# Two-stream attention block: the query features move to the other stream's fourth PSUM bank, and ScalarE's order of two activations is swapped

## What is computed

```
q, k, v = out@Wq+bq, out@Wk+bk, out@Wv+bv            # split into 16 heads of 8
favor(x) = [exp(u - h), exp(-u - h)] / sqrt(8)        # u = xs@omega, h = 0.5*sum(xs*xs), xs = x * 8**-0.25
Qf, Kf = favor(q), favor(k)
S_t = S_{t-1} + Kf_t v_t^T;  z_t = z_{t-1} + Kf_t     # causal, over the 1024 tokens
a_t = (Qf_t S_t) / (Qf_t z_t + 1e-6)
h = LN(out + a@Wo + bo);  out = LN(h + relu(h@W1+bf1)@W2 + bf2)
```

## Time and profile before

| | |
|---|---|
| median of 3 runs | 2047.53 us (2046.19 to 2049.01) |
| profiled execution, its own time | 2053.53 us |
| its span, first to last instruction | 2051.6 us |
| busy, share of the span | PE 82%, DVE 76%, POOL 48%, ACT 43%, PEld 61% |
| mean granted TensorE clock | 0.903 of full speed |
| attention slots | about 641 to 1880 us of the span |

### The profile page before, as it was taken

How to read it: one execution, slowest core, us unless ns; L and a number is a source line. 1 busy time by engine, 2 the same in 40 slices (tenths; PEclk the granted TensorE clock), 3 DMA queues, 4 the chain that set the end, 5 groups by cost and what they waited for, 6 DMA issues and landing times. The chain is left out here.

```text
span 2051.6 us, 69397 instructions
## 1 busy us (share of the span) xinstructions
PE 1680.2 (82%) x28443; PEld 1259.8 (61%) x28445; DVE 1554.3 (76%) x3835; ACT 883.3 (43%) x1642; POOL 983.6 (48%) x1045
## 2 busy tenths in 40 slices
PE   5655555469937999999999989999989999995798
PEld 4332334359935666766666766666766666663798
DVE  2899965359976878878888878888868878885675
ACT  2555555446623444444444434444434444442321
POOL 0677747769953224234234224224224224223797
PEclk7877765579977999999999999999999999997899
DMA  7400011122230000000000000000000000000001
GB/s 202 86 0 0 0 24 34 34 63 63 64 111 2 3 3 3 3 3 3 3 3 3 3 4 3 3 3 3 3 4 3 3 3 3 3 3 1 16 31 37
DMA packets 60732, 42.92 MB, mean 21 GB/s; under 512 B 19720, under 2 KB 54800, under 8 KB 59952
## 3 DMA queue, kind: packets, MB, share of 16 engines
q1 hardware_dynamic: 47504, 25.35, 4.7%
q0 software_dynamic: 4352, 8.99, 1.3%
q10 hardware_dynamic: 8608, 4.67, 0.9%
HBM read 24.22 MB, written 14.77 MB: 19 GB/s over the span
## 5 line engine op out<-in xcount | busy, mean ns | idle before, releaser
L368 POOL TENSOR_TENSOR at_rstd<-at_mv,const 128x4 f32<-128x4 f32 x96 | 19.5, 203 | 570.0 <-DVE at_mv L362 569.9
L1622 PE MATMUL psum<-attn_w,at_qa 128*128 128x128 f32 x1536 | 184.1, 278 | 0.0
L1614 PE MATMUL psum<-at_vT,attn_w 128*128 128x512 f32 x384 | 180.5, 613 | 1.4 <-ACT at_vT L1427 0.9
L1622 PEld LDWEIGHTS psum<-attn_w,at_qa 128*128 128x128 f32 x1536 | 175.2, 192 | 2.7 <-issue 0.6
L1431 ACT ACTIVATE at_qa<-psum,attn_bf 128x512 f32<-128x512 f32 x192 | 132.0, 687 | 90.2 <-PE psum L1614 90.2
L1326 DVE TENSOR_SCALAR at_kb<-at_kf,const 128x512 f32<-128x512 f32 x192 | 157.9, 882 | 0.0
L1332 DVE STREAM_TRANSPOSE at_vb<-at_vT 32x512 uint32<-32x512 uint32 x192 | 134.7, 702 | 1.9
L1848 PE MATMUL psum<-tilesT,ti_masked 128*128 128x128 f32 x1024 | 119.9, 279 | 12.9 <-POOL ti_masked L1810 12.9
L1848 PEld LDWEIGHTS psum<-tilesT,ti_masked 128*128 128x128 f32 x1024 | 117.8, 195 | 14.6 <-issue 14.6
L1556 PE MATMUL psum<-at_state,at_qa 64*64 64x36 f32 x3072 | 116.8, 242 | 9.6 <-issue 9.2
L1435 ACT ACTIVATE at_qa<-at_qf,const 128x512 f32<-128x512 f32 x192 | 122.3, 710 | 0.0
(11 more groups left out here) (303 smaller groups left out, 4315.2 us busy)
## 6 DMA issues: line engine op xcount, KB each, us to landing
ex_xs<-sorted_x SPq DMA_DIRECT2D x80, 65.0 KB
x<-in_L_attn_x ACTq DMA_DIRECT2D x8, 512.0 KB, 8.5
ex_feats<-token_y SPq DMA_DIRECT2D x4, 1024.0 KB, 8.1
out<-x SPq DMA_DIRECT2D x16, 256.0 KB, 2.3
expert_w<-in_L_ffn_w SPq DMA_DIRECT2D x1, 2048.0 KB, 9.5
attn_w<-in_L_attn_W SPq DMA_DIRECT2D x2, 768.0 KB
token_y<-ex_y,ex_place POOLq DMA_INDIRECT x72
sorted_x<-ex_spare SPq DMA_DIRECT2D x1, 1040.0 KB, 8.3
```

Source lines behind the costliest of these rows:

```text
L1614: mm(bank(f.s, c), k.w1[:, f.l, c * P:(c + 1) * P], hT[f.s][:], start=True, stop=True).then_inc(hid_ready, 1)
L1622: last = mm(bank(f.s, 1)[:, c * D:(c + 1) * D], hidden[f.s][:, t, c * P:(c + 1) * P], k.w2[:, f.l, t, :], start=(t == 0 and c == 0), stop= ...
```

## The change

Two things are changed in `attention`. The query features are accumulated in `bank(1 - s, 3)`, the fourth bank of the other stream, in place of `bank(s, 3)`. With that, `sums` no longer writes to the bank that the exponential reads, and PE's wait for `qf_ready` moves from before the first sums to before the fourth hidden product, the next write to that bank. On ACT the copy of the transposed rows (`hT`) comes ahead of the query exponential. No arithmetic is added or removed.

```diff
@@ ScalarE @@
                         act.wait_ge(kt_ready, n + 1)
                         nc.scalar.activation(flat(kt[s][:]), bank(s, 2), ACT.Copy).then_inc(vk_taken, 1)
+                    if f:
+                        act.wait_ge(hT_ready, f.count + 1)
+                        nc.scalar.activation(hT[f.s][:], bank(f.s, 2), ACT.Identity, bias=col(B1, f.l), scale=col(G1, f.l)).then_inc(hT_taken, 1)
+                    if a:
                         act.wait_ge(feat_ready, n * 2 + 2)
                         if l == 0 and a.before:
                             act.wait_ge(outcome_free, a.turn - 1)
-                        nc.scalar.activation(qf[s][:], bank(s, 3), ACT.Exp, bias=feature_bias[:, 0, l:l + 1]).then_inc(qf_ready, 1)
-                    if f:
-                        act.wait_ge(hT_ready, f.count + 1)
-                        nc.scalar.activation(hT[f.s][:], bank(f.s, 2), ACT.Identity, bias=col(B1, f.l), scale=col(G1, f.l)).then_inc(hT_taken, 1)
+                        nc.scalar.activation(qf[s][:], bank(1 - s, 3), ACT.Exp, bias=feature_bias[:, 0, l:l + 1]).then_inc(qf_ready, 1)
@@ TensorE @@
-                        mm(bank(s, 3), wu[0][:, l, :], xT[s][:], start=True, stop=False)
+                        mm(bank(1 - s, 3), wu[0][:, l, :], xT[s][:], start=True, stop=False)
...
                         pe.wait_ge(kq_taken, n * 2 + 2)
-                        mm(bank(s, 3), cst(k, "half"), sqq[s][:], start=False, stop=True).then_inc(feat_ready, 1)
+                        mm(bank(1 - s, 3), cst(k, "half"), sqq[s][:], start=False, stop=True).then_inc(feat_ready, 1)
...
                         pe.wait_ge(vk_taken, n * 2 + 2)
-                        pe.wait_ge(qf_ready, n + 1)
                         sums(s, 0)
                         sums(s, 1)
                     if f:
                         pe.wait_ge(hT_taken, f.count + 1)
                         for c in range(GC):
+                            if a and c == 3:
+                                pe.wait_ge(qf_ready, n + 1)
                             mm(bank(f.s, c), k.w1[:, f.l, c * P:(c + 1) * P], hT[f.s][:], start=True, stop=True).then_inc(hid_ready, 1)
```

## The result

| | before | changed |
|---|---|---|
| median of 6 runs each, same chip | 2048.27 us (2045.37 to 2053.09) | 2038.34 us (2031.34 to 2040.28) |
| profiled execution, its span, mean clock | 2053.53, 2051.6, 0.903 | 2037.89, 2036.0, 0.908 |

The ratio is 0.9943, with the 95% interval from 0.9923 to 0.9962: faster, by 9.9 us of medians. The forecast was 2041.3 us in a range of 2036.0 to 2047.0, for a gain of 6.2. That is a ratio of 0.9970, which lies just outside the interval: the gain was larger than forecast, and not by noise alone. Two later comparisons gave the changed kernel 0.9931 and 0.995 of the kernel before, and one of the kernel before against itself gave 1.0003.

What follows compares the result with a forecast made beforehand. PE was taken to bound attention (1111.82 of 1187.00 us busy). 26 ordinary slots x 0.24 us = 6.2 us, set against the median before of 2047.53 us, gave 2041.3 us, range 2036.0 to 2047.0.

Steps and rivals of the forecast that it cites:

- An ordinary slot: Attention slot outside the groups bound by POOL and DVE: hidden product starts 0.24 us earlier, in 26 of 47 slots.
- The exponential and the new wait: On ACT and PE: later exponential still precedes the ReLUs, and the wait before the fourth hidden product is met; cost nothing.
- The groups of three: Seven groups, 21 attention slots, held by DVE and POOL at 52.24 us from first to third normalisation: no gain.
- holes for issue: PE's idle stretches in dense runs of small passes, 0.8 us on average; may open or close, counted as nothing.
- All slots gaining: Rival: groups of three not bound, all 47 slots give 0.24 us, 11.3 us in all, 2036.2 us; chance 0.09.
- Swallowed: Rival: copy starts no earlier or holes take the gain back; 2.6 us down to nothing, 2044.9 to 2047.5; chance 0.26.
- slower: Rival: shifted instruction stream opens new 0.8 us holes in ordinary slots, 10.4 us against 6.2, 2051.7 us; chance 0.08.
- (1): PE in attention: the first sums no longer wait for ACT and start right behind the transposes.
- (2): ACT in attention: the copy of the rows starts 0.05 us behind the transposes, ahead of the exponential.
- (5): Ordinary slots 0.24 us shorter; groups of three still 52.2 us from first to third normalisation, PE waiting longer for rows there.
- (3): Hidden product 0.05 us behind the copy, with new PE waits for the copy of about 0.1 us per ordinary slot.
- (6): PE's holes for issue keep the same total; the prediction is wrong if this fails by more than some us.

Runs made afterwards that it cites:

- number 2: Changed kernel with ACT's old order (exponential first, then the copy), bank and PE wait as changed: 2037.44 us, ratio 0.9982.
- number 1: Kernel before with ACT's order alone swapped (copy, then exponential), bank and PE wait as before: 2127.7 us, ratio 1.0422.
- number 8: Changed kernel with PE's wait for the query exponential before the first hidden product in place of the fourth: 2065.7 us, ratio 1.007.
- number 9: Changed kernel with POOL's two residual passes moved behind the feed-forward input's passes and held until DVE's masked copies are made: 2025.77 us, ratio 0.9905.
- number 3: Changed kernel with one more, long-met wait on PE before the first sums in each slot: 2036.41 us, ratio 0.9972.
- number 4: Kernel before without PE's wait for the copy of the transposed keys ahead of the sums: 2043.14 us, ratio 1.0006.
- number 6: Changed kernel with POOL's two residual passes moved behind the first reciprocal deviation and the two passes after it, without a hold: 2098.73 us, ratio 1.023.
- number 10: Changed kernel with POOL's residual passes moved later, these and the feed-forward input's passes held until DVE's masked copies are made: 2027.39 us, ratio 0.992.

## Why the prediction was right, and what it missed

**An ordinary slot: right.** Predicted 0.24 us, with the copy 0.05 behind the transposes and the hidden product 0.05 behind the copy; measured 0.24, with 0.04 and 0.05. The two halves are shown apart by the floor: the bank gives 0.10 (number 2), the swap the other 0.14, and only behind the bank (number 1). That the two differences of 0.10 and 0.14 come out to the hundredth owes something to luck, since they were read from ends that the profile models. Of PE's 18.7 us of waits the 26 ordinary slots give back 6.2.

**The exponential and the new wait cost nothing: right.** The first ReLU is 1.16 us behind the first product and 0.64 behind the exponential. There is no wait before the fourth product. Number 8 shows what it would cost without cover.

**The groups of three give nothing: right in the slots that bind.** The steps are 26.11 us as before. The 21 slots together took 540.9 to 542.6 us against 541.2 to 544.9, which overlaps. That POOL's queue is what holds them was read from the earlier trace rows and is shown by number 9. "Nothing of PE is in it" was too strong: number 8 shows that a hidden product 0.67 us later lengthens the steps.

**The total: 3.7 us too little.** The unknown beside the sum, holes for issue, was left at nothing, and this is the term that was too small. Two parts of it are seen. The hole of 2.19 us in the earlier trace rows, seven passes before the end, and the hole in slot 10 both went with the one wait fewer on PE in each slot, and both came back in number 3. They are worth up to 2.0 us and some 1.6 us. The prediction had the first in hand and said that such a hole might close. With both the sum is 9.8 us, beside 9.9, 14.7 and 8.6 measured, and number 3, without them, gave 5.5 beside 6.2.

That the sum now meets the measured 9.9 so well is luck as much as account, for number 4 does not fit: it has neither hole, and its median is no shorter than that of the kernel before. In the profiles, slots 1 to 46 take 1177.0 us as the mean of the three kernels with the old floor, and 1168.4 for the changed kernel's three and number 3. Of these 8.5 us, 6.0 is the floor of 25 slots, 0.6 lies over the floor and 1.9 in the groups, both less than the 3 to 4 us by which executions of one kernel differ there. What makes the gains of 8.6 to 14.7 us differ so from chip to chip is not settled.

The Trainium skill, page "Runtime: NRT & Kernel Launch", section "Instruction fetch mechanics", has the crossing between blocks of instructions as mostly hidden. Holes of 1.8 and 2.19 us that come and go with one instruction in each slot do not fit that. That they lie whole multiples of 256 records apart speaks for blocks of a fixed length, though no run here shows what PE does at such a place.

**The rivals.** All slots gaining (2036.2 us) is nearer to the measured 2038.34 than the forecast is, and yet the trace rules it out: the steps of the groups did not move. The total alone would have picked the wrong theory. Swallowed is out by the floor, slower by the sign.

**What the profile after would show.** Points (1), (2), (4) and (5) are as written. In (3) the wait for the copy is 0.18 us, not about 0.1. In (6) the total before the weighted part is 25.2 us against 23.9, so it held as a total. It hides that single holes moved: the one in slot 10 went while others were longer, and the one in slot 47 lay outside the stretch looked at.

## What to carry to other kernels

A wait that is taken away is worth only the time until the next releaser of the work behind it: here 0.10 of 0.43 us, until the next one was moved too. Sort the slots by what holds them, and judge by the length of one slot without holes, since it repeats to 0.01 us where the whole scatters by several. The other side of this is that the floor alone does not give the whole: here holes in the instruction stream moved too. If a second engine's queue holds some slots, moving its passes can pay, but look at what the other engine does at the new place: the same two passes of POOL made the kernel 2.3% slower in one place and gave the best one, 2025.77 us, in another.

## What the runs showed of the hardware that was not expected

**DVE beside POOL.** The masked copies by kernel (shortest, median, longest in ns, of 192): changed, number 6, number 10.

```profile
L1326 DVE TENSOR_SCALAR at_kb<-at_kf,const x192: 472/476/1494, 638.4 to 1831.1; 128x512 f32<-128x512 f32 x192
```

```profile
L1326 DVE TENSOR_SCALAR at_kb<-at_kf,const x192: 477/1487/1516, 637.6 to 1898.5; 128x512 f32<-128x512 f32 x192
```

```profile
L1326 DVE TENSOR_SCALAR at_kb<-at_kf,const x192: 475/479/486, 639.1 to 1823.0; 128x512 f32<-128x512 f32 x192
```

A copy of 0.48 us alone takes up to 1.5 us beside a POOL pass, while POOL's pass goes from 1.27 to at most 1.46. In slot 27 of the changed kernel the copies that start at 1321.84 and 1322.88 us each end 0.28 us behind the end of the POOL pass beside them (1322.68 and 1324.09), and the two copies after that, with no pass beside them, take 0.47 us. The Trainium skill, page "SBUF — State Buffer", section "SBUF: two separate sides", says that GpSimd and some DVE instructions (those in a mode that takes two ports, or with two inputs in SBUF) take a shared port pair as an exclusive lock, so that the later one is blocked until the other is done. The trace agrees in that each slow copy ends only behind its POOL pass. In which mode the copies run, no run here shows.

**The clock.** Without the bank, PE is idle for 1.54 us in each slot of 25.4 before the sums. The granted clock then fell to 0.50 (1.2 GHz) in the stretch shown, and in 20 of 47 slots the hidden product took longer, by 34 us in all. With 0.43 us idle in a slot, as before the change, the stretch stays at 0.99, and with 0.85 us (number 8) three stretches between 800 and 1800 us are at 0.99 to 1.00. A wait can so cost more than its length. Why 20 slots had it and 27 with the same wait did not is not settled.

**Holes tied to the place in the instruction stream.** In the written-out slots 1 to 10 all 31 holes for issue over 0.5 us lie 11 or 12 records behind a multiple of 256 in PE's queue. One wait more or less in each slot so puts in or takes out single idle stretches of 1 to 2.2 us: one in slot 10, one in slot 47. Both profiled executions of the kernel before had both, as had number 3, and none of the changed kernel had either.
